# First chunks loaded ahead of the edge lists, and one-hots from pairs, in a GAT and relational graph layer kernel

## The reference

```
h  = x @ W
e  = exp(-leaky_relu((h@a_l)[src] + (h@a_r)[dst], 0.1))
hp = segment_sum(e * h[dst], src) / (segment_sum(e, src) + 1e-5)
x1 = layernorm(x + elu(hp))

u  = x1 @ root + bias
for r in range(8):
    mask = (edge_type == r)
    mean = segment_sum(x1[src] * mask, dst) / max(segment_sum(mask, dst), 1)
    u = u + mean @ weight[r]
z   = concat([u, x1]) @ w_gate + b_gate
out = layernorm(x1 + tanh(u) * z + x1 * (1 - z))
```

## Time and profile before

| | before |
|---|---|
| runs, us | 1102.37, 1100.87, 1101.48; median 1101.48 |
| the profiled execution's own time, us | 1096.03 |
| its span, first to last instruction, us | 1094.2 |
| mean granted TensorE clock over the span | 0.984 |
| busy: PE, PE weight loads, DVE, ACT, POOL | 94%, 78%, 31%, 26%, 23% |
| first matmul of x @ W; first count matmul of window 0, us | 14.65; 48.14 |
| windows stage until about, us | 217 |

### The profile page before, as it was taken

One profiled execution on the slowest core, in us unless ns is written; L12 is line 12 of the kernel. 1 busy time (PEld: TensorE's weight loads), 2 busy tenths in 40 slices (PEclk: granted clock), 3 DMA queues, 4 the chain that ended last, 5 costly groups with the idle time before them and its releaser, 6 DMA issues.

```text
span 1094.2 us, 14960 instructions
## 1 busy us (share of the span) xinstructions
PE 1032.7 (94%) x5454; PEld 852.1 (78%) x5454; DVE 341.7 (31%) x707; ACT 279.6 (26%) x478; POOL 253.6 (23%) x196
## 2 busy tenths in 40 slices
PE   5899878996999999999999999999999999999995
PEld 3565546775889889889889889889889889888874
DVE  7976665370112102112112012012012112022285
ACT  3322243383111211212112121222122121122422
POOL 0000000106331321321321311321321321326720
PEclk9999999998999999999999999999999998999998
DMA  5213334507421141141141141141141141212302
GB/s 211 77 40 107 97 97 125 162 1 270 143 79 33 38 147 30 39 138 39 39 138 39 39 136 41 39 138 39 39 138 39 39 138 39 68 41 75 125 1 94
DMA packets 63621, 91.81 MB, mean 84 GB/s; under 512 B 4115, under 2 KB 30178, under 8 KB 63428
## 3 DMA queue, kind: packets, MB, share of 16 engines
q1 hardware_dynamic: 63556, 90.86, 25.8%
HBM read 75.17 MB, written 15.67 MB: 83 GB/s over the span
## 4 chain that ended last, share of the span: by engine, by line
PE 83%; DVE 9%; issue 3%; ACT 3%; POOL 1%; DVEq 1%; DMA 0%; SPq 0%; ACTq 0%
PE ps L1035 18%; PE ps L1036 18%; PE ps L1037 18%; PE ps L1223 9%; PE ps L1224 9%; PE ps L1099 4%; PE ps L1062 2%; PE ps L1212 2%; DVE hot L824 2%; DVE oh_s L756 2%; POOL x_lo L437 1%; DVE ps L967 1%; DVE ps L966 1%; DVE w_lo L751 1%; PE ps L1070 1%
## 5 line engine op out<-in xcount | busy, mean ns | idle before, releaser
L416 POOL TENSOR_TENSOR w_lo<-w_raw,w_hi 128x512 fp32r<-128x512 f32 x168 | 216.7, 1293 | 746.7 <-ACT w_hi L478 548.2
L478 ACT CAST w_hi<-w_raw 128x512 fp32r<-128x512 f32 x184 | 114.3, 621 | 490.8 <-PE ps L1037 424.2
L1035 PE MATMUL ps<-w_hi,M_hi 128*128 128x512 f32 (+1 forms) x560 | 223.1, 398 | 17.3 <-POOL w_lo L416 9.4
L1036 PE MATMUL ps<-w_hi,M_lo 128*128 128x512 f32 (+1 forms) x560 | 219.6, 392 | 0.0
L1037 PE MATMUL ps<-w_lo,M_hi 128*128 128x512 f32 (+1 forms) x560 | 219.6, 392 | 0.0
L917 DVE SCALAR_TENSOR_TENSOR u<-ps,scale,u 128x512 f32<-128x512 f32 (+1 forms) x90 | 66.4, 745 | 427.3 <-PE ps L1037 427.3
L1223 PE MATMUL ps<-C_hi,x_hi 128*128 128x320 f32 (+3 forms) x640 | 190.5, 315 | 0.0
L1224 PE MATMUL ps<-C_hi,x_lo 128*128 128x320 f32 (+3 forms) x640 | 189.4, 313 | 0.0
L1036 PE MATMUL ps<-w_hi,M 128*128 128x512 f32 (+1 forms) x360 | 142.5, 396 | 0.0
L1037 PE MATMUL ps<-w_lo,M 128*128 128x512 f32 (+1 forms) x360 | 142.4, 396 | 0.0
L1035 PE MATMUL ps<-w_hi,M 128*128 128x512 f32 (+1 forms) x360 | 142.3, 395 | 0.0
(11 more groups left out here) (152 smaller groups left out, 765.0 us busy)
## 6 DMA issues: line engine op xcount, KB each, us to landing
w_raw<-weights SPq DMA_DIRECT2D x184, 256.0 KB, 2.7
C_dram<-Cst SPq DMA_DIRECT2D x25, 512.0 KB, 6.0
C_hi<-C_dram SPq DMA_DIRECT2D x8, 1600.0 KB, 7.3
z<-b_gate SPq DMA_DIRECT2D x5, 512.0 KB, 9.8
u<-bias SPq DMA_DIRECT2D x5, 512.0 KB, 7.3
xT_raw<-xT SPq DMA_DIRECT2D x8, 312.5 KB, 7.3
u<-x SPq DMA_DIRECT2D x4, 512.0 KB, 4.9
last_raw<-weights SPq DMA_DIRECT2D x8, 256.0 KB, 4.9
```

The source lines that it names most:

```text
L416: pool.tensor_tensor(w_lo[k % RING][:, :], w_raw[k % RING][:, :], w_hi[k % RING][:, :].bitcast(f32), ALU.subtract).then_inc(w_lo_done, 1)
L478: nc.scalar.copy(w_hi[k % RING][:, :], w_raw[k % RING][:, :]).then_inc(w_hi_done, 1)
L1035: mm(o, lhs_hi[:, k, c], w_hi[k % RING][:, :], start=opens, stop=False)
L1036: mm(o, lhs_lo[:, k, c], w_hi[k % RING][:, :], start=False, stop=False)
```

## The change

SP issues W chunk 0 and xT chunk 0 first and then the four lists; the rest of the order stays. DVE works on the limits in three pieces, `unit_limits`, `edge_keys` and `window_limits`, each after the low parts of one chunk; the eight one-hot instructions are spread anew, four of them after the last low parts. PE runs the spreading of the diagonals after chunk 0 and the transpose of the limits after chunk 5. The source within its tile, `src_h`, is stored twice side by side, and the one-hot compares pairs of neighbouring columns with that pair: the same 2560 outputs per instruction. Of the three splits of the second half before the windows, two move behind the loops of windows 0 and 1.

```diff
@@ -113,7 +113,7 @@
                 ints = sb("ints", [P, 3, TILES], i32, setup)
                 src_tile = sb("src_tile", [P, TILES], i32, setup)
                 src_in = sb("src_in", [P, TILES], i32, setup)
-                src_h = sb("src_h", [P, ALL_TILES], f16, setup)
+                src_h = sb("src_h", [P, ALL_TILES, 2], f16, setup)
@@ -327,14 +327,15 @@
                 sp.dma_start(C_hi[:, :, :].bitcast(f32), C_dram[ds(i, 1), :, :, :].rearrange("o m p n -> p (o m) n"))\
                   .then_inc(c_here, 16)
 
-            sp.dma_start(units_i[:, :], dst_units).then_inc(edges_here, 16)
-            sp.dma_start(ints[:, 0, :], dst_cols).then_inc(edges_here, 16)
-            sp.dma_start(ints[:, 1, :], src_cols).then_inc(edges_here, 16)
-            sp.dma_start(ints[:, 2, :], type_cols).then_inc(edges_here, 16)
             for k in range(KT):
                 if k < RING:
                     load_chunk(0, k, first=True)
                 sp.dma_start(xT_raw[:, k, :], xT[k * P:(k + 1) * P, :]).then_inc(xT_here[k], 16)
+                if k == 0:
+                    sp.dma_start(units_i[:, :], dst_units).then_inc(edges_here, 16)
+                    sp.dma_start(ints[:, 0, :], dst_cols).then_inc(edges_here, 16)
+                    sp.dma_start(ints[:, 1, :], src_cols).then_inc(edges_here, 16)
+                    sp.dma_start(ints[:, 2, :], type_cols).then_inc(edges_here, 16)
             sp.dma_start(a_bc[:, :], a[0, :].partition_broadcast(P)).then_inc(a_here, 16)
             load_ahead(0)
             load_ahead(1)
@@ -705,7 +706,7 @@
             v.memset(eps_col[:, :], EPS)
             v.memset(mv[:, :, :], 1.0)
             v.memset(scale[0][:, :], 1.0)
-            v.memset(src_h[:, :], 0.0)
+            v.memset(src_h[:, :, :], 0.0)
             v.memset(key[:, :], -1.0)
             v.memset(y_sq[:, :], 1.0)
             step(v.memset(dots[:, :], 0.0))
@@ -714,58 +715,77 @@
             v.tensor_scalar(ident_r[:, :], iota_s[:, :], part_col[:, :], None, ALU.is_equal)
             v.tensor_scalar(win_edge[:, 0:1], part_col[:, :], float(WIN), None, ALU.mult)
             step(v.tensor_scalar(win_edge[:, 1:2], part_col[:, :], float(WIN), float(WIN - 1), ALU.mult, ALU.add))
-            dve.wait_ge(edges_here, 64)
-
...
-            def one_hots(t0, t1):
+            def one_hots(c):
+                t0, t1 = ALL_TILES * c // KT, ALL_TILES * (c + 1) // KT
                 n = t1 - t0
-                v.tensor_tensor(oh_s[:, t0 * P:t1 * P].rearrange("p (t s) -> p t s", s=P),
-                                iota_s[:, :].unsqueeze(1).broadcast_to([P, n, P]),
-                                src_h[:, t0:t1].unsqueeze(2).broadcast_to([P, n, P]), ALU.is_equal).then_inc(oh_done, 1)
-
-            for k in range(KT):
-                if k == 1:
-                    dve.wait_ge(lohi_turned, 1)
-                    v.tensor_copy(lohi_row[:, :], ps[0:1, 6 * H2:6 * H2 + WINDOWS]).then_inc(row_done, 1)
+                v.tensor_tensor(oh_s[:, t0 * P:t1 * P].rearrange("p (t a b) -> p t a b", a=P // 2, b=2),
+                                iota_s[:, :].rearrange("p (a b) -> p a b", b=2).unsqueeze(1).broadcast_to([P, n, P // 2, 2]),
+                                src_h[:, t0:t1, :].unsqueeze(2).broadcast_to([P, n, P // 2, 2]), ALU.is_equal).then_inc(oh_done, 1)
+
+            def lows(k):
                 dve.wait_ge(xT_hi_done, k + 1)
                 v.tensor_tensor(M_lo[0][:, k, 0:N], xT_raw[:, k, :], M_hi[0][:, k, 0:N].bitcast(f32), ALU.subtract)\
                  .then_inc(xT_lo_done, 1)
                 split_low(0, k)
-                one_hots(ALL_TILES * k // KT, ALL_TILES * (k + 1) // KT)
+
+            def unit_limits():
+                dve.wait_ge(edges_here, 64)
...
+                d.then_inc(units_diag_done, 1)
+
+            def edge_keys():
+                v.tensor_scalar(src_in[:, :], ints[:, 1, :], P - 1, None, ALU.bitwise_and)
+                step(v.tensor_scalar(src_tile[:, :], ints[:, 1, :], 7, None, ALU.arith_shift_right))
+                v.tensor_copy(src_h[:, 0:TILES, :], src_in[:, :].unsqueeze(2).broadcast_to([P, TILES, 2]))
+                step(v.scalar_tensor_tensor(code_f[:, :], src_tile[:, :], float(R), ints[:, 2, :], ALU.mult, ALU.add))
+                step(v.scalar_tensor_tensor(key[:, 0:TILES], code_f[:, :], 1.0 / (P // 2), ints[:, 0, :], ALU.mult, ALU.add))
+
+            def window_limits():
+                dve.wait_ge(units_bcast, 1)
...
+                v.tensor_tensor(lohi[:, 7:8], lohi[:, 5:6], lohi[:, 6:7], ALU.add).then_inc(lohi_done, 1)
+
+            lows(0)
+            unit_limits()
+            lows(1)
+            edge_keys()
+            lows(2)
+            one_hots(0)
+            lows(3)
+            window_limits()
+            lows(4)
+            one_hots(1)
+            lows(5)
+            one_hots(2)
+            lows(6)
+            dve.wait_ge(lohi_turned, 1)
+            v.tensor_copy(lohi_row[:, :], ps[0:1, 6 * H2:6 * H2 + WINDOWS]).then_inc(row_done, 1)
+            one_hots(3)
+            lows(7)
+            for c in range(4, KT):
+                one_hots(c)
             dve.wait_ge(row_done, 1)
 
             def low_h(t):
@@ -792,8 +812,7 @@
                 v.tensor_tensor(h_part(1, 1, t, rows(t)), o, h_part(0, 1, t, rows(t)).bitcast(f32),
                                 ALU.subtract).then_inc(u_drained, 1)
 
-            for k in range(RING - 1):
-                split_low(1, k)
+            split_low(1, 0)
 
             def leaky(j):
                 dve.wait_ge(sum_done, j + 1)
@@ -823,6 +842,8 @@
                         dve.wait_ge(counted[SLOT_BEFORE[s]], n)
                         v.tensor_scalar(hot[:, SLOT[s] * NP:(SLOT[s] + 1) * NP], table[:, :], float(WIN * w),
                                         key[:, ds(tile + s, 1)], ALU.add, ALU.is_equal).then_inc(built[s], 1)
+                if w < RING - 2:
+                    split_low(1, w + 1)
                 for k in range(RING - 1, KT):
                     if w == SPLIT_AT[k] + 1:
                         split_low(1, k)
@@ -1020,15 +1041,6 @@
                 if SLOT_BEFORE[s] >= s:
                     pe.sem_inc(counted[SLOT_BEFORE[s]], 1)
 
-            pe.wait_ge(units_diag_done, 1)
-            for c in range(2):
-                last = mm(ps[0:WINDOWS, (4 + c) * H2:(4 + c) * H2 + SUB * UNITS], ones[0:UNITS, 0:WINDOWS],
-                          unit_diag[:, c, :, :].rearrange("u s v -> u (s v)"), start=True, stop=True)
-            last.then_inc(units_bcast, 1)
-            pe.wait_ge(lohi_done, 1)
-            mm(ps[0:1, 6 * H2:6 * H2 + WINDOWS], lohi[:, 7:8], ident[0:WINDOWS, 0:WINDOWS],
-               start=True, stop=True).then_inc(lohi_turned, 1)
-
             def product_item(k, t, lhs_hi, lhs_lo, opens, closes_, to=None):
                 c = slice(t * P, t * P + rows(t))
                 o = bank(t if to is None else to, rows(t))
@@ -1049,8 +1061,22 @@
                     pe.wait_ge(u_drained, NT * half + t + 1)
                 product_item(k, t, M_hi[0], M_lo[0], k == 0, k == KT - 1, to=xw_bank(t))
 
-            for i in range(ALL):
-                xw_item(0, *divmod(i, NT))
+            def chunk_items(*ks):
+                for k in ks:
+                    for t in range(NT):
+                        xw_item(0, k, t)
+
+            chunk_items(0)
+            pe.wait_ge(units_diag_done, 1)
+            for c in range(2):
+                last = mm(ps[0:WINDOWS, (4 + c) * H2:(4 + c) * H2 + SUB * UNITS], ones[0:UNITS, 0:WINDOWS],
+                          unit_diag[:, c, :, :].rearrange("u s v -> u (s v)"), start=True, stop=True)
+            last.then_inc(units_bcast, 1)
+            chunk_items(1, 2, 3, 4, 5)
+            pe.wait_ge(lohi_done, 1)
+            mm(ps[0:1, 6 * H2:6 * H2 + WINDOWS], lohi[:, 7:8], ident[0:WINDOWS, 0:WINDOWS],
+               start=True, stop=True).then_inc(lohi_turned, 1)
+            chunk_items(6, 7)
 
             def turn_counts(j, part, blocks=None):
                 m0, m1 = turn_blocks(part)
```

More of the change, by code:

```diff
@@ L716, in _ @@
             step(v.tensor_scalar(win_edge[:, 1:2], part_col[:, :], float(WIN), float(WIN - 1), ALU.mult, ALU.add))
-            dve.wait_ge(edges_here, 64)
-            tiles_i = units_i[:, :].rearrange("u (s e) -> u s e", s=SUB)
-            v.tensor_reduce(unit_mm[:, 0, :], tiles_i, X, ALU.max)
-            step(v.tensor_reduce(unit_mm[:, 1, :], tiles_i, X, ALU.min))
-            for c in range(2):
-                for h in range(SUB):
-                    d = v.tensor_scalar(unit_diag[:, c, h, :], ident[0:UNITS, 0:UNITS], unit_mm[:, c, h:h + 1], None, ALU.mult)
@@ L725, in _ @@
[L725 to L741, removed]
-            step(v.tensor_scalar(reach[:, 0, 0:ALL_TILES // BODY], iota_body[0:WINDOWS, :], lohi[:, 4:5], None, ALU.is_lt))
-            step(v.tensor_reduce(lohi[:, 5:6], reach[:, 0, 0:ALL_TILES // BODY], X, ALU.add))
@@ L744, in _ @@
```

(14 more changed lines are left out.)

14 lines of the change are left out of this document (13 added, 1 removed).

## The result

| | before | after |
|---|---|---|
| median of the first comparison, us (4 runs each) | 1101.92 | 1094.37 |
| median of a second one, 23 and 12 runs | 1101.1 | 1095.19 |
| ratio after to before, 95% interval | | 0.9935 [0.9917, 0.9952]; 0.9948 [0.9925, 0.9970] |
| profiled execution's own time; span, us | 1096.03; 1094.2 | 1095.78; 1094.0 |
| first matmul of x @ W; first, last count matmul, us | 14.65; 48.14; 200.5 | 6.67; 40.62; 194.4 |

The change is faster by 5.9 to 7.6 us, 0.5 to 0.7%; forecast were 8.0 and a time of 1093.5. The two profiled spans are equal within 0.2 us, which at first sight says that nothing was gained. But the profiled execution of before is an odd one: its own time lies 5 us under the median of its runs. The first experiment is about that.

What follows compares the result with a forecast made beforehand. VectorE was taken to set the start, up to the first count matmul at 48.14 us. 9.0 earlier, less 0.2 for splits and 0.8 for a clock fall, gave 8.0 off the median 1101.48: 1093.5, range 1090.5 to 1097.8.

Steps and rivals of the forecast that it cites:

- First transfers: Start of the product: first W and xT chunks land at 3.35 and 4.15, PE starts at 6.3 rather than 14.65.
- The same set of transfers up to xT1, so chunk 1 at 12.2: Second pair of loads: xT1 copied at 10.72 as before, low parts of chunk 1 ready at 12.2; lists at 8.6.
- One-hot 1.40 apart: One-hots on DVE: pairs give two outputs per step, 1.40 us each rather than 2.73; bounds 0.96 and 2.73.
- Rival (a): One-hots on DVE: pairs bring nothing, still 2.73 us each, first count matmul at 47.6, about 1101 us; chance 0.09.
- Rival (b): One-hots on DVE: inner runs of two make it pause, 4.05 us each, start 10.3 later, 1111.5 us; chance 0.03.
- New wait of 2.2 for the transpose, on the path: DVE before its last one-hots: waits from 27.3 to 29.5 for PE's transpose of the limits, other work queued behind.
- First count matmul 39.1, 9.0 earlier: Start of the windows: first count matmul at 39.1 rather than 48.14, so 9.0 us earlier.
- 0.2 given back in window 1: Windows 0 and 1: the moved splits mostly hide in DVE's idle time, costing 0.2 us in window 1.
- 0.8 for a clock fall before the windows, 0 or 1.6: PE gap from 36.3 to 39.1: the granted clock may fall, costing 1.6 us; half, 0.8, taken, ends 0 and 1.6.
- Rival (c): Start of the product: first pair lands late or clock stays low, gain only 3.5 us, 1098.0 us; chance 0.16.
- (d): Stage before the windows: one-hots at 0.96 us and no clock fall, gain 10.8 us, 1090.7 us; chance 0.15.

Runs made afterwards that it cites:

- The first experiment: The kernel before, unedited, run and profiled once more: median 1102.67 us, ratio to before 1.001 [0.9985, 1.0035].
- the trace with PE kept busy: After, with ten extra 128x512 matmuls into a free bank between product and windows: 1094.8 us, ratio to before 0.9933 [0.9908, 0.9959].
- experiment 3: After, with the pair edits undone, so one-hots from a single key element again: median 1103.6 us, ratio to before 1.0029 [1.0010, 1.0049].
- experiment 5: After, with PE's transpose of the window limits behind chunk 3 instead of chunk 5: median 1091.05 us, ratio to before 0.9895 [0.9858, 0.9931].
- the second profiles: Before and after, each unchanged and profiled again: medians 1102.67 us (before) and 1095.19 us (after, 12 runs, ratio 0.9948).

## Why the prediction was right, step by step

The forecast was 8.0 us and 1093.5; measured are 7.6 and 5.9 us, 1094.37 and 1095.19, both inside the forecast range of 1090.5 to 1097.8. The mechanism was the one forecast: the order and the pairs together make PE the bound, and a wait for the transpose is left. The gain was a little too large. By its own steps:

- *First transfers*: start of PE 6.67 for 6.3, since xT landed 0.24 later than counted.
- *The same set of transfers up to xT1, so chunk 1 at 12.2*: the step that failed. It was ready at 13.3. The set of transfers was the same and still its last part came 1.1 us later; that the same bytes land by the same time, whatever their order, was the wrong assumption. The lists too came at 9.73, not 8.6. Also chunk 0 took 5.91 for 5.29: the fast clock came 4.9 us after PE's start (at 11.6), not 3.7. Either alone would have moved chunk 1 to near 13.3, and the trace with PE kept busy tells them apart. There the clock rose 2.9 us after PE's start, chunk 0 and the diagonals were done early, and chunk 1 still had to wait for its data:

```profile
13.01 0.50 PE L1047 MATMUL ps<-w_hi,M_hi 128*128 128x512 f32 x1 [0.78 <-DVE w_lo L720]
```

  How soon the clock rises is no constant either: 3.7 and 5.7 us after PE's start in the two profiles of before. This step is the 1.1 us by which the transpose, and all behind it, came late.
- *One-hot 1.40 apart*: measured 1.40 (15.93 to the next at 17.34; four in 5.67). Rival (a), pairs that bring nothing, is out. Its case, the order with single keys, is experiment 3: the first count matmul came 0.5 later where I had 0.5 earlier. Rival (b) is out.
- *New wait of 2.2 for the transpose, on the path*: 2.33, and experiment 5 took it away for 2.6 at the start.
- *First count matmul 39.1, 9.0 earlier*: 40.62, 7.5 (7.8 between the second profiles). Of the 1.5 missing 1.1 is the step above; DVE goes on from the transpose at 30.86, not 29.6, and the first build reaches the first count matmul in 0.72, not 0.57, since PE's own start behind the last one-hot (zero matmuls at 40.16, 0.79 after it) now ends last.
- *0.2 given back in window 1*: 0.2 to 0.3 up to window 2. At the end of the windows it is no longer there: from the first to the last count matmul before takes 152.4, and after 153.8 with its fall of 1.47, so 152.3 without it.
- *0.8 for a clock fall before the windows, 0 or 1.6*: it was there in one profile of after (1.47) and not in the other.

So the windows end 7.5 us earlier without that fall and 6.1 with it (200.5 to 194.4). The two comparisons give 7.6 and 5.9, with intervals of 5.3 to 9.1 and 3.3 to 8.3. That they lie within 0.4 and 2.1 of the forecast 8.0 is in part luck: the start fell short by 1.5, and the scatter of the runs is larger than that. Rival (c) was right in kind and small, 1.1 us and not 3.7; but what came late was the second pair, not the first.

Some details of the forecast are loose without bearing on it: (c) comes to 1098.0, just outside the range that is said to reach through it; (d) comes to 1090.7; and in (b) a start 10.3 later would be 1111.8, not 1111.5.

## What to carry to other kernels

Put first what has the longest chain behind it, but look at what it pushes back, and at how many partitions each transfer has. A reorder alone was worth nothing here and a faster instruction alone about half; only together did they give the whole. Where the granted clock falls in some executions and not in others, read a small change at the instruction where its stage ends, and try whether thin matmuls can be kept from standing together: spreading the 25 of each relation was worth more here (9.8 us) than the whole change.

## What the runs showed of the hardware that was not expected

- A comparison of two 16-bit tensors took 2.81 us for 2560 elements with one key element read 128 times, and 1.49 with a pair of equal keys read 64 times.
- Falls of the granted clock to 0.50 lasted 3.4, 6.8 or 10.2 us, in a few cases longer, and differed between executions of the same kernel: 27.3 us behind the windows in one, 37.5 in another. Runs of one kernel spread over up to 12 us (1092.8 to 1104.9 for the pairs alone), and the slow ones are those with the lower mean clock: of 27 runs of before the fastest (1095.91) had 0.985, the slowest (1105.19) 0.973.
- A 79-row transfer of 79 KB moved its rows one behind another for 4.2 us and kept the lists behind it back by 2.1 us; cut in 64 and 15 rows it was done in 0.9.
- 44 more matmuls ahead of a loop brought three waits of some 4.3 us each, hundreds of us later, one at each return of the loop, with an instruction packet landing in each.
